# A fused adapter kernel on one core: a new order for its first tiles of work, another order of its first loads, and one subtraction given to GpSimd

## What is computed

```python
def reference(x, thresholds, deltas, zero_points, labeler_index, router_w, A, B, W, lora_A, lora_B_w, gate, kernel, bias, ...):
    # quantise: each value by the group of its threshold, 0 beyond all of them
    q = where(gi == G, 0, (clip(round(x / d) + zp, 0, 63) - zp) * d)
    # gated adapters: the two best of four experts, softmax of their logits
    x = x + einsum('te,teo->to', gates, einsum('ter,eor->teo', q @ A, B)) * 4
    # dense layer with the adapter of the sequence's label
    y = x @ W.T + (x @ lora_A[label]) @ lora_B_w.T * 0.5
    # dense layer, bias, adapters mixed by the gate, and a shared adapter
    return x + y @ kernel + bias + adapters(y)
```

## Time and profile before

| what | value |
|---|---|
| median of 3 runs | 464.24 us (463.82 to 464.54) |
| the profiled execution | 463.36 us, of which the span of the profile is 461.6 us |
| TensorE busy | 448.9 us (97% of the span) |
| VectorE busy | 392.6 us (85%) |
| ScalarE busy | 357.6 us (77%) |
| GpSimd busy | 9.3 us (2%) |
| mean granted clock of TensorE | 0.989 of full speed (2.4 GHz); it is at 1.0 or at 0.5 |

### The profile page before, as it was taken

One profiled execution on the slowest core, in us unless ns is written; L12 is line 12 of the kernel. 1 busy time (PEld: TensorE's weight loads), 2 busy tenths in 40 slices (PEclk: granted clock), 3 DMA queues, 4 the chain that ended last, 5 costly groups with the idle time before them and its releaser, 6 DMA issues.

```text
span 461.6 us, 5629 instructions
## 1 busy us (share of the span) xinstructions
PE 448.9 (97%) x2166; PEld 350.3 (76%) x2166; DVE 392.6 (85%) x392; ACT 357.6 (77%) x296; POOL 9.3 (2%) x11
## 2 busy tenths in 40 slices
PE   8889599999999999999999999999999999999997
PEld 8767477888888887777877877787778777867884
DVE  1587499999889999999799999999996999899410
ACT  1459999974697989799799988789697899778002
POOL 0000001000010000000010000000000000000000
PEclk9899799999999999999999999999999999999999
DMA  7998436220444250325107108015215014101102
GB/s 248 342 353 348 93 80 177 75 57 1 110 154 147 92 109 29 114 92 159 57 1 250 58 1 236 15 59 159 98 51 159 1 58 138 50 9 45 47 1 91
DMA packets 36124, 50.35 MB, mean 109 GB/s; under 512 B 26658, under 2 KB 26914, under 8 KB 33826
## 3 DMA queue, kind: packets, MB, share of 16 engines
q1 hardware_dynamic: 35090, 42.66, 29.4%
q0 software_dynamic: 1008, 7.34, 4.8%
HBM read 39.51 MB, written 10.49 MB: 108 GB/s over the span
## 4 chain that ended last, share of the span: by engine, by line
PE 88%; ACT 4%; SPq 3%; DMA 3%; issue 1%; ACTq 0%
PE bank L1088 13%; PE bank L1090 13%; PE bank L1089 13%; PE bank L971 6%; PE bank L1065 6%; PE bank L999 6%; PE bank L1030 6%; PE bank L1025 6%; PE bank L1026 6%; PE bank L940 5%; DMA xq<-xt_in 3%; PE bank L1086 2%; PE bank L995 2%; ACT level L427 2%; PE bank L1006 1%
## 5 line engine op out<-in xcount | busy, mean ns | idle before, releaser
L680 DVE COPY_PREDICATED val<-inside,val 128x2048 f32<-128x2048 uint8 x56 | 142.5, 2546 | 0.3
L440 ACT ACTIVATE val<-level,shift,small 128x2048 f32<-128x2048 int16 x64 | 134.0, 2093 | 10.0 <-PE bank L971 9.9
L427 ACT ACTIVATE level<-xq,inv 128x2048 int16<-128x2048 f32 x64 | 127.9, 1998 | 5.6 <-DMA xq<-xt_in 5.1
L1088 PE MATMUL bank<-p_hi,x_hi 128*128 128x512 f32 x256 | 103.0, 402 | 0.0
L1090 PE MATMUL bank<-p_hi,x_lo 128*128 128x512 f32 x256 | 100.1, 391 | 0.0
L1089 PE MATMUL bank<-p_lo,x_hi 128*128 128x512 f32 x256 | 100.1, 391 | 0.0
L662 DVE TENSOR_SCALAR val<-val,width,unshift 128x2048 f32<-128x2048 f32 x64 | 87.0, 1359 | 6.4 <-ACT val L440 6.3
L671 DVE TENSOR_SCALAR inside<-absx,thr 128x2048 uint8<-128x2048 f32 x56 | 72.6, 1296 | 0.0
L1088 PEld LDWEIGHTS bank<-p_hi,x_hi 128*128 128x128 f32 x256 | 48.1, 188 | 17.6 <-issue 9.0
L1089 PEld LDWEIGHTS bank<-p_lo,x_hi 128*128 128x128 f32 x256 | 48.1, 188 | 10.5 <-issue 0.7
L1090 PEld LDWEIGHTS bank<-p_hi,x_lo 128*128 128x128 f32 x256 | 48.1, 188 | 10.5
(11 more groups left out here) (98 smaller groups left out, 449.9 us busy)
## 6 DMA issues: line engine op xcount, KB each, us to landing
xs<-xt_in SPq DMA_DIRECT2D x8, 1024.0 KB, 4.9
wst<-w_in SPq DMA_DIRECT2D x14, 512.0 KB, 4.2
xq<-xt_in POOLq DMA_DIRECT2D x7, 1024.0 KB, 6.9
out_t<-ost SPq DMA_DIRECT2D x14, 512.0 KB, 3.3
la<-la_in SPq DMA_DIRECT2D x4, 512.0 KB, 5.6
kst<-k_in SPq DMA_DIRECT2D x4, 512.0 KB, 12.9
lb<-lb_in SPq DMA_DIRECT2D x4, 512.0 KB, 15.3
kst<-k_in SPq DMA_DIRECT2D x1, 2048.0 KB, 10.4
```

The costliest lines, as they stand in the source:

```text
L427: nc.scalar.activation(level[:, g % 2], xq[:, c % 2], ACT.Copy, scale=inv[:, group(g)]).then_inc(levels_made, 1)
L440: nc.scalar.activation(val[:, turn(c, g)], level[:, g % 2], ACT.Relu, bias=shift[:, group(g)], scale=par[:, 1, group(g)]).then_inc(raised, 1)
L680: nc.vector.copy_predicated(val[:, acc(c)], inside[:, g % 2], val[:, turn(c, g)]).then_inc(merged, 1)
L1088: mm(o, x_hi[:, s, k, at], p_hi[:, h, k], start=False, stop=False)
```

## The change

It alters the following, and nothing of what is computed.

1. `keep_warm` issues 5 products and not 7. The first quarter of `la` comes as two transfers of half the columns, with a semaphore each (`lora_first`).
2. SyncE's list: `bw` ahead of `ab`; W's first tile ahead of all of K's quarters; x of sequence 0 and W's second tile ahead of the reading of the labels and so of `alt`. `lb` keeps its place behind all of these.
3. TensorE starts `u_product(0)` ahead of the `k_update`s: two products, six `k_update`s, six products, two `k_update`s.
4. ScalarE rounds W's first tile ahead of K's row blocks; `u_out(0)`, `p_out(0)`, the first two `rows_out`, `u_out(1)` and `weight_hi(2)` are written into the list ahead of the loop of steps, between the quantising of sequence 0, and in later steps `u_out` stands ahead of the groups.
5. The remainder of W's first tile is taken by GpSimd, ahead of its loads of `xq`; VectorE's list loses it. `weight_lo(1)` waits for it, so that the count stays in order.
6. `TAKEN` and `LAGS`: in slots 1 to 8 the groups go 1, 0, 2, 2, 2, 1, 1, 1 and not 0, 2, 2, 2, 2, 1, 1, 0, and from slot 9 on they are where they were. `mid(0)` moves from step 6 to step 7, `mid(1)` from behind step 15 to behind step 14, and gate steps of sequences 0 to 4 move by one slot.
7. The last `k_update` of the second half stands two row blocks later within step 7.

```diff
-WARM, WARMUPS = 256, 7
+WARM, WARMUPS = 256, 5
...
-    LAGS = [(2, 4, 5, 6, 7, 9), (3, 3, 4, 5, 5, 6), (3, 4, 4, 5, 6, 7), (3, 5, 5, 6, 7, 9), (2, 5, 5, 6, 7, 8), (2, 3, 3, 3, 4, 5), (1, 2, 2, 4, 4, 5), (2, 2, 3, 3, 4, 6)]
-    TAKEN = [0, 0, 2, 2, 2, 2, 1, 1, 0, 1, 1, 1, 1, 1, 1, 1, 1, 2]
+    LAGS = [(2, 4, 5, 6, 7, 9), (2, 3, 3, 4, 4, 5), (3, 4, 4, 5, 6, 8), (3, 6, 6, 7, 8, 10), (2, 5, 5, 6, 8, 9), (2, 3, 3, 3, 4, 5), (1, 2, 2, 4, 4, 5), (2, 2, 3, 3, 4, 6)]
+    TAKEN = [0, 1, 0, 2, 2, 2, 1, 1, 1, 1, 1, 1, 1, 1, 1, 1, 1, 2]
...
+            pool.wait_ge(w_hi_made, 1)
+            nc.gpsimd.tensor_tensor(w_lo[0], wst[0], w_hi[0].bitcast(F32), ALU.subtract).then_inc(w_lo_made, 1)
...
-            for g in range(NG):
+            for h in range(HALVES):
+                at = slice(h * HALF, (h + 1) * HALF)
+                sp.dma_start(la[:, 0, at], a["la"][:, 0, at]).then_inc(lora_first[h], 16)
+            for g in range(1, NG):
                 sp.dma_start(la[:, g], a["la"][:, g]).then_inc(lora_in[g], 16)
+            sp.dma_start(bw, a["bw"]).then_inc(bw_in, 16)
             sp.dma_start(ab_raw, a["ab"]).then_inc(ab_in, 16)
-            sp.dma_start(bw, a["bw"]).then_inc(bw_in, 16)
+            sp.dma_start(wst[0], w_v[0]).then_inc(w_in[0], 16)
             for i in range(KPARTS):
-                if i == KPARTS // 2:
-                    sp.dma_start(wst[0], w_v[0]).then_inc(w_in[0], 16)
...
+            sp.dma_start(xq[:, 0], x_v[0]).then_inc(x_first_in, 16)
+            sp.dma_start(wst[1], w_v[1]).then_inc(w_in[1], 16)
             sp.wait_ge(itok_in, 16)
...
-            sp.dma_start(wst[1], w_v[1]).then_inc(w_in[1], 16)
-            sp.dma_start(xq[:, 0], x_v[0]).then_inc(x_first_in, 16)
...
-                    if h == 0 and o == 4:
-                        weight_hi(0)
...
+            weight_hi(0)
             kp_split(0)
...
             weight_hi(1)
+            u_out(0)
+            p_out(0)
+            for i in range(HALVES):
+                rows_out(i)
             magnitude(0)
             levels(0, 1)
+            u_out(1)
             raise_levels(0, 1)
+            weight_hi(2)
             levels(0, 2)
...
+                if m == 1:
+                    dve.wait_ge(w_lo_made, 1)
...
-                    if h == 0 and o == 1:
-                        weight_lo(0)
...
                 for o in range(KT):
+                    if n == 0 and o == 2:
+                        pe.wait_ge(ab_lo_made, 2)
+                        for k in range(len(kfirst)):
+                            k_update(0, k)
                     mm(ubank[n], wst[n % 2][:, o], aefft[:, o], start=o == 0, stop=False)
...
+                    else:
+                        for k in range(len(kfirst), KT):
+                            k_update(0, k)
```

More of the change, by code:

```diff
@@ L170, in build @@
     ones_made, bias_hi_made, bias_made, taken = sem("ones_made"), sem("bias_hi_made"), sem("bias_made"), sem("taken")
+    lora_first = [sem(f"lora_first{h}") for h in range(HALVES)]
     lora_in = [sem(f"lora_in{g}") for g in range(NG)]
@@ L566, in _, with p_out @@
             act.wait_ge(tables, 1)
+            def p_out(n):
+                act.wait_ge(ofull, n + 1)
+                h, i = n // KT, tile_of(n)
+                nc.scalar.activation(p_hi[:, h, i], obank[n % RING], ACT.Copy).then_inc(p_hi_made, 1)
             levels(0, 0)
@@ L930, in _ @@
             last.then_inc(cfull, 1)
-            pe.wait_ge(ab_lo_made, 2)
-            for o in range(KT):
-                k_update(0, o)
             def u_product(n):
@@ L1032, in _ @@
                         last.then_inc(kp_read, 1)
-                    if n == KT - 1 and o == KT // 2:
+                    if n == KT - 1 and o == KT - 2:
                         k_update(1, n)
```

23 lines of the change are left out of this document (9 added, 14 removed).

## The result

| kernel | median | lowest to highest | executions | ratio to the kernel before (95% interval) |
|---|---|---|---|---|
| before, same chip | 464.09 us | 463.82 to 464.54 | 4 | |
| changed | 459.39 us | 457.31 to 462.06 | 4 | 0.9907 (0.9882 to 0.9932) |
| changed, later on another chip (before there 463.44) | 460.43 us | 455.19 to 461.88 | 12 | 0.9918 (0.9892 to 0.9944) |

The account below looks back on a forecast made before the run. The prediction took TensorE, 97% busy, as the bound, with its wait for `ust` the main loss: 5.1 + 2.1 = 7.2 us off 464.24, start and GpSimd at 0, gave 457.0 us, range 455.5 to 459.7.

Parts of the forecast that it names:

- The stall and its half clock: TensorE's wait for `ust` ahead of `u_product(2)`, 5.1 us, plus 2.1 us of slow products behind it: 7.2 us to win.
- By ScalarE's list: ScalarE's reordered list copies `ubank` 1 by 39.7, 6.4 us ahead of need, so the whole 7.2 us goes.
- the term of the transfers' order: SyncE's queue: the same transfers stand ahead of `lb` in another order, so the tables gain 0.
- All this still holds if x lands as late as now: ScalarE's list before `u_product(2)`: the 7.2 us gain was claimed not to depend on x landing earlier.
- The start is worth nothing: Step 0 ends 2 to 3 us earlier, but the tables still wait for `lb` at 33.3: gain 0.
- The halved first transfer with it, at 0: First quarter of `la` in halves: counted with the five warm-up products in the start's whole gain, 0.
- the cover of 2 to 3 us: Ahead of the tables: step 0 done 2 to 3 us sooner than now, while TensorE waits for `alt` and `lb`.
- GpSimd at 0: GpSimd's subtraction for W's first tile, estimated at 2.25 us, is hidden by 6 us before step 0: cost 0.
- Rival 4: Step 0 waits for GpSimd's subtraction: beyond 9.7 us the excess is paid, slower from 16.9; chance 0.04 with other losses.
- Rival 1: The new hole from about 30.2 to 33.3 throttles TensorE, `u_product(1)` takes 2.1 us more: 459.1 us, chance 0.26.
- Rival 2: `w_lo` of step 2, with 2.2 us to spare, or another list entry becomes the wait: 458 to 460 us, chance 0.11.
- Rival 3: Transfers get better in the new order and `lb` lands at 32.1: 455.8 us, chance 0.06.

Follow-up runs that it names:

- e2: Changed kernel with the first quarter of `la` as one whole transfer again, five warm-up products kept: 455.49 us, ratio 0.9832.
- e6: Kernel before with only ScalarE's list, `TAKEN`, `LAGS` and the last `k_update`'s place from the changed one: 459.34 us, ratio 0.9917.
- e11: e2 run again, on another chip: 456.27 us, ratio 0.9848.
- e8: e2 with the transfers in the order of the kernel before: 458.63 us, ratio 0.9899.
- e1: Changed kernel with 7 warm-up products again, the halved first transfer kept: 457.9 us, ratio 0.9871.
- e4: Changed kernel with two filler products on TensorE ahead of each later quarter of `la`: 458.58 us, ratio 0.9892.
- e10: Changed kernel run again unaltered, on another chip: 460.43 us, ratio 0.9918.
- e14: Changed kernel with TensorE waiting for both halves before its first product of `la`: 460.19 us, ratio 0.9907.
- e7: e2 with the remainder of W's first tile back on VectorE: 456.2 us, ratio 0.9826, three of seven executions near 464 us.
- e15: e7 with 7 warm-up products instead of 5: 456.12 us, ratio 0.9838.
- e13: Changed kernel with the first transfer halved by partitions, rows whole, TensorE waiting for both: 462.33 us, ratio 0.9957.

## Why the prediction was right, and where it was wrong

**The stall and its half clock: right, and in place.** No wait for `ust`, the second `ust` 5.8 us ahead of need (6.4 forecast), `u_product(2)` in 3.62 us. Where nothing disturbs it (e2), the second `ust` is at 38.67 (39.7 forecast), `u_product(2)` at 44.78 instead of 51.20, and the span is 8.5 us shorter. Of these, 5.1 + 2.2 are the term of the sum, with 5.82 - 3.62 for the half clock; 0.7 is `lb`, which lands that much earlier, within the 1.2 that the forecast left open; the last 0.5 is step 1. It follows the start of `u_product(1)` after 3.92 us in e2 (33.71 to 37.63) and after 4.39 before, where it waited for its remainder:

```profile
38.82 0.50 PE L1025 MATMUL bank<-kp_hi,w_hi 128*128 128x512 f32 x1 [0.23 <-DVE w_lo L703]
```

The forecast had `u_product(2)` at 46.1 and took TensorE's work from 34.43 to there as unchanged.

**"By ScalarE's list": half wrong.** The sum gave the whole 7.2 us to the lists. e6 gives them 3.9. That e2 and e11, with `la` whole, come out at 7.1 to 7.8, near the 7.2, is in part luck: the lists' term was too large and the term of the transfers' order, put at 0, too small by about as much. "All this still holds if x lands as late as now" is the sentence that failed: it was worked out for the second `ust` and there it holds (41.92 in e6, needed at 45.12). It was not worked out for `w_lo` of step 2, the place that the same part named as the narrowest, with 2.2 us to spare. With x at 31.27 that place is 3.2 us later and waits 1.26 us.

**"The start is worth nothing": right for the tables, wrong for x.** The tables wait for `lb` as forecast. With step 0 done early, TensorE waits for `alt` and `lb` at 31.59 and 32.63 in e2 (forecast 32.1 and 33.3). But the transfers' order also brings x 6.6 us forward (31.2 in e6, 24.6 in e2), and by e6 and e8 that is worth some 3 us.

**"The halved first transfer with it, at 0": the step that made the forecast wrong.** Two things stood behind it. First, that the very same transfers stand ahead of `lb`, so that it lands as before. It does in the profile of the changed kernel (33.3), but in e1 and e4, at the same bytes, it lands at 36.6 to 37.1. The rate of the queue was taken as given, and from 4 to 8 us it is 240 to 303 GB/s and not 376 to 400. Nor is `lb` issued earlier, as "the queue is fed earlier" has it: at 18.2 before, at 20.0 in the changed kernel, at 18.7 in e2. Second, that anything lost at the start lies in the cover of 2 to 3 us. The cover was right, and too small for 13 us at half clock in the products of `la` and `bw`, which alone lose 6.5 us. It covers nothing of a late `alt` or `lb`. The forecast even had the price, "each microsecond of the start would count in full", but as the price of a case to which it gave no chance. A smaller piece that lands earlier seemed harmless. In the profile of the changed kernel TensorE starts earlier on work that then runs out, and in all of them what follows in the queue comes more slowly. The measured price of the halves is 464 times the difference of the ratios: 0.0075 (0.9907 - 0.9832) or 0.0070 (0.9918 - 0.9848), 3.2 to 3.5 us, with 1.7 to either side. The miss is 2.9 us by the first ratio and 3.4 by the second, so the halves account for all of it within the noise.

**GpSimd at 0: right, with its size.** 2.34 us, over at 23.26, within the 6 us of cover. The estimate from the Trainium skill (GPSIMD Engine Reference, section 3.1) was 2.25, and the traces agree within 6% (2.34 to 2.39 us in the thirteen profiles that have it). Rival 4 has no part in it. What the forecast didn't price is that VectorE can be held up meanwhile (below).

**Rival 1: the mechanism exists, mostly in other places.** The hole of 1.29 us ahead of `alt` costs no clock in e2; one of 3.12 us does in e1, where the clock is 0.50 from 38 to 40. And in the changed kernel's profile it was the hole inside `la` that took the clock, and then the 1.91 us ahead of step 0, which took it in e10 and e14 too. The forecast looked at neither, though its own first part names two small waits at the start and slow products behind one of them.

**Rival 2** is a wait of 0.4 us in the changed kernel, and the main loss in e6 and e8. **Rival 3** happened in e2 by 0.7 us. The moves of `mid`, the gate steps and the last `k_update` cost nothing that shows there: TensorE is busy 60.00 of 60 and 80.00 of 80 us from 60 to 200 in e2. TensorE's new order at the start (part 3 of the change) and the earlier rounding of W's first tile were not tried by themselves.

## What to carry to other kernels

Splitting the first transfer so that an engine can begin sooner wasn't free here: the engine may begin on work that runs out, and what stands behind it in the queue may come later. Try the split alone, and look at the spread of the executions as well as at one profile. When a gain is laid to one part of a change, work out each later wait under the old state of the other parts, the narrowest one first. And before a hole is filled, ask what will be late next: here two fills moved the wait from 31 us to 47 and beyond, and brought nothing.

## What the runs showed of the hardware

- **A halved first transfer slows the queue.** From 4 to 8 us it moves 240 to 325 GB/s, in seven profiles, and 376 to 400 with it whole. It does so with 64 partitions of whole rows as well as with half rows. The DMA engines are about as full in both (a share of 0.85 to 1.00, and of 1.00 to 1.02), so they are occupied about as long and move fewer bytes. How late the later loads land differs between profiles: the first quarter of `lb` at 33.1 and 33.3 in two profiles of the changed kernel, at 37.1 in e1, where the same bytes stand ahead of it.
- **TensorE's products can take twice their time with a granted clock of 1.00 in the record** (e7, one profile: 217 ns for each product of 64 columns, 113 in e15). Only the durations show it, so products of one shape should be compared beside the clock.
- **The length of a hole alone doesn't decide whether the clock falls.** Behind 1.19 us among the 64-column products it was at 0.50 for 13 us, behind 0.62 us (e10) it wasn't, behind two of 0.47 us (e13) it was. All thirteen profiles with GpSimd's subtraction have a wait of 1.9 us ahead of step 0. Behind it the clock was at 0.50 for a piece of step 0 in four of them (the changed kernel, e8, e10, e14), and in e2 it was at 1.00 throughout. What makes the difference no run here tells.
- **GpSimd's subtraction held up VectorE's beside it, in the one profile where they meet.** Two subtractions of VectorE, over 32 partitions, in the changed kernel, the second beside GpSimd's 20.92 to 23.26, and the second one in e2, where it runs alone:

```profile
L814 DVE TENSOR_TENSOR ab<-ab_raw,ab 32x512 fp32r<-32x512 f32 x1 | 2.8, 2806 | 0.0
L814 DVE TENSOR_TENSOR ab<-ab_raw,ab 32x1024 fp32r<-32x1024 f32 x1 | 1.2, 1215 | 0.0
```

```profile
L811 DVE TENSOR_TENSOR ab<-ab_raw,ab 32x512 fp32r<-32x512 f32 x1 | 0.7, 683 | 0.0
```

The same operation takes 2.81 us and not 0.68. The columns are busy us and mean ns of one. The Trainium skill (GPSIMD Engine Reference, section 1, Specifications) says that GpSimd shares its interfaces to SBUF with VectorE and contends with instructions of two SBUF inputs; the trace agrees, by these 2.1 us. It agrees on the other side too: in e2 VectorE's additions of a bank in PSUM to `kst`, with one SBUF input, start 0.6 us behind GpSimd's subtraction (17.87 to 20.26) and take 3.68 us for six, as in e15, where GpSimd has no such work.

```profile
18.44 3.68 DVE L726 TENSOR_TENSOR kst<-bank,kst 128x512 f32<-128x512 f32 x6 [0.68 <-PE bank L905]
```

In the changed kernel's profile nothing waited for the 2.1 us.
